# The half copy of a1_rows on GpSimd moved ahead of the product of bias and b1

## The reference

```
x = x + (x @ W.T + bias + (x @ A0[id0].T) @ B0[id0].T)      # W 512x512; A0 32 x 16 x 512; B0 32 x 512 x 16
x = x + (x @ B1[id1].T) @ A1[id1].T                         # B1 8 x 16 x 512;  A1 8 x 512 x 16
```

## Time and profile before

| | |
|---|---|
| median of 3 runs | 102.09 us (100.86 to 102.17) |
| the profiled execution | 100.96 us |
| its span, first to last instruction | 98.8 us |
| mean granted clock of TensorE in the span | 0.983 of full speed |
| busy: PE / PEld / DVE / ACT / POOL | 93% / 92% / 65% / 59% / 59% |

### The profile page before, as it was taken

The page is one execution under the profiler, slowest core; times in us unless marked ns, Lnnn a source line. Parts: engine busy times, 40 slices in busy tenths (PEclk is TensorE's granted clock), DMA queues, the critical chain, the costliest instruction groups (busy, mean ns, idle before and its releaser), DMA issues.

```text
span 98.8 us, 2305 instructions
## 1 busy us (share of the span) xinstructions
PE 92.2 (93%) x662; PEld 91.1 (92%) x662; DVE 64.5 (65%) x120; ACT 58.7 (59%) x189; POOL 57.9 (59%) x126
## 2 busy tenths in 40 slices
PE   5979999999992999999999999999999999999980
PEld 5979989998991999999999999999999999999970
DVE  4499796254172527786876859587876959687360
ACT  0074679695464829695957658494856749490310
POOL 6504003980277999897585958567595957618500
PEclk9999999999999589999999999999999999999999
DMA  1999999927688158979999389995537192620205
GB/s 47 345 360 380 380 338 299 213 55 194 180 231 267 47 133 224 277 288 243 218 234 245 127 209 255 224 251 211 99 141 177 69 239 36 211 106 0 106 0 212
DMA packets 16335, 19.45 MB, mean 197 GB/s; under 512 B 1444, under 2 KB 11556, under 8 KB 16164
## 3 DMA queue, kind: packets, MB, share of 16 engines
q1 hardware_dynamic: 15040, 14.04, 48.0%
q0 software_dynamic: 1280, 5.28, 21.4%
q10 hardware_dynamic: 4, 0.00, 0.0%
HBM read 13.47 MB, written 5.84 MB: 195 GB/s over the span
## 4 chain that ended last, share of the span: by engine, by line
PE 64%; issue 14%; POOL 8%; DMA 8%; SPq 2%; DVE 1%; DVEq 0%; POOLq 0%
PE psum L394 48%; PE psum L440 12%; DMA gathered_rows<-by_rank,rows 4%; PE psum L432 4%; DMA by_rank<-row_ends 3%; SPq L182 2%; POOL a_by_rank L285 2%; POOL bias_b_terms L282 1%; POOL w_chunks L277 1%; DVE y L679 1%; POOL g_sel L332 1%; POOL g_sel L270 0%; DVE y L769 0%; DVEq L44 0%; POOL batch_mask L267 0%
## 5 line engine op out<-in xcount | busy, mean ns | idle before, releaser
L394 PE MATMUL psum<-wd,xt 128*128 128x256 f32 (+1 forms) x384 | 63.2, 314 | 0.0
L394 PEld LDWEIGHTS psum<-wd,xt 128*128 128x128 f32 x384 | 57.0, 191 | 0.0
L558 ACT ACTIVATE wd<-table_rounded 128x128 fp32r x128 | 27.7, 298 | 14.3 <-PE psum L394 12.4
L339 POOL TENSOR_TENSOR up_rows<-gathered_rows,up_rows 128x512 fp32r<-128x512 f32 x16 | 20.7, 1292 | 15.1 <-ACT up_rows L558 15.1
L322 POOL DMA_INDIRECT gathered_rows<-by_rank,rows x16 | 15.9, 994 | 6.8 <-DMA by_rank<-row_ends 4.3
L640 DVE TENSOR_TENSOR xt<-psum,xt 128x512 fp32r<-128x512 f32 x16 | 11.1, 693 | 6.7 <-ACT xt L558 6.7
L440 PE MATMUL psum<-up_rows,u_sel 128*128 128x256 f32 x96 | 14.8, 292 | 0.0
L647 DVE STREAM_TRANSPOSE psum<-x_squares 128x512 f32<-128x512 f32 x13 | 14.4, 1109 | 0.0
L440 PEld LDWEIGHTS psum<-up_rows,u_sel 128*128 128x128 f32 x96 | 13.5, 199 | 0.1
L332 POOL TENSOR_TENSOR g_sel<-gathered_rows,batch_mask 128x16 f32<-128x16 f32 x64 | 12.1, 225 | 0.9 <-DMA gathered_rows<-by_rank,rows 0.6
L558 ACT ACTIVATE xt<-psum 128x512 fp32r<-128x512 f32 x16 | 9.6, 598 | 4.9 <-DVE psum L647 2.2
(11 more groups left out here) (60 smaller groups left out, 71.1 us busy)
## 6 DMA issues: line engine op xcount, KB each, us to landing
out<-y SPq DMA_DIRECT2D x15, 256.0 KB
x_squares<-in_x SPq DMA_DIRECT2D x8, 256.0 KB, 6.1
w_rows<-in_L_cond_base_weight SPq DMA_DIRECT2D x4, 256.0 KB, 3.6
bw_rows<-in_L_cond_lora_B_w SPq DMA_DIRECT2D x1, 1024.0 KB, 6.8
a_rows<-in_L_cond_lora_A_w SPq DMA_DIRECT2D x1, 1024.0 KB, 9.1
by_rank<-bw_by_rank SPq DMA_DIRECT2D x4, 256.0 KB
x_squares<-in_x SPq DMA_DIRECT2D x8, 128.0 KB, 3.2
x_rows<-in_x SPq DMA_DIRECT2D x3, 256.0 KB, 9.2
```

What stands on the lines that cost most here:

```text
L339: nc.gpsimd.tensor_tensor(out=up_rows[:, k % 2, LO, :], in0=gathered_rows[:, k % GATHERS, 0:D], in1=up_rows[:, k % 2, HI, :], op=ALU.subtr ...
L394: last = nc.tensor.matmul(bank_of(k, half)[:, start:end], xt[:, k % 2, c, x_part, :], wd[:, w_part, c, col:col + end - start], start=(c == ...
L558: return nc.scalar.activation(dst, src, ACT.Copy)
```

## The change

On GpSimd the wait for a1_rows and the half copy by rank change places with the waits for the bias and b1 and their product. Nothing else differs.

```diff
             nc.gpsimd.tensor_copy(w_chunks[:, C - 1, :, :],
                                   w_rows[:, C - 1, :].rearrange("p (m c) -> p c m", c=C)).then_inc(w_chunked[C - 1], 1)
 
+            pool.wait_ge(a1_in, 16)
+            nc.gpsimd.tensor_copy(a1_by_rank[:, R // 2:R, :],
+                                  a1_rows[:, :, R // 2:R].rearrange("p o r -> p r o")).then_inc(a1_by_rank_ready, 1)
             pool.wait_ge(bias_in, 16)
             pool.wait_ge(b1_in, 16)
             nc.gpsimd.tensor_tensor(out=bias_b1_terms[:, :], in0=b1_rows[:, :], in1=bias_all[:, :],
                                     op=ALU.mult).then_inc(bias_b1_step, 1)
-            pool.wait_ge(a1_in, 16)
-            nc.gpsimd.tensor_copy(a1_by_rank[:, R // 2:R, :],
-                                  a1_rows[:, :, R // 2:R].rearrange("p o r -> p r o")).then_inc(a1_by_rank_ready, 1)
```

## The result

The changed kernel takes 98.36 us (median of 4 executions, 97.92 to 98.58), the kernel before 102.13 (100.86 to 103.36); ratio 0.9665, 95% interval 0.9568 to 0.9762. Two later comparisons gave 98.35 and 98.38 us with ratios 0.9771 (0.9715 to 0.9828) and 0.9834 (0.9778 to 0.9891). The ratio moves because the kernel before has executions of 99.6 and of 103.7 us, and the comparisons leave out most of the long ones; the experiments take that apart. The profiled execution took 97.92 us, span 95.8, against 100.96 and 98.8: 3.04 us less.

What follows compares the result with a forecast made beforehand. A start-up of about 32 us, then a loop that TensorE fills, was taken as the bound. Hole 1.89 plus clock 2.09 less 0.57 gave 3.41: 100.96 to 97.55 us, forecast 97.9 with part of the spread; range 96.9 to 99.9.

Steps and rivals of the forecast that it cites:

- Where the copy could start: GpSimd's half copy, waiting only for a1_rows, starts at about 14.5 us in place of 17.73.
- The product within 0.1 us of 16.5: GpSimd's product, now behind the copy, still starts near 16.52 us when the bias comes; latest bound 17.15.
- What is late next: ScalarE's copy of g caps the row_ends store on SyncE: issue at about 20.38, 2.02 us earlier, not 2.50.
- Landings unchanged: The row_ends store's landing and gather(0) keep their 3.37 and 4.11 us in their new place.
- A: TensorE's hole shrinks but stays: landing 0.5 to 1.6 us longer in the crowd, clock falls; 99.5 to 100.6 us; chance 0.12.
- D: Slower: DMA crowd makes row_ends store and gather take 6.1 us each; 103.7 us, or 105.8; chance 0.03.
- The hole, 1.89 us: TensorE's idle time before add_gh(0), 29.96 to 31.85, closes, with 0.13 us to spare: 1.89 us gained.
- The clock, 2.09 less 0.57: TensorE's stretch behind the hole runs at full clock: 2.09 us back, less 0.57 lost waiting for GpSimd.
- GpSimd's lateness: TensorE waits for g_sel(1), up_low(1) and g_sel(2) in the first blocks: 0.14, 0.15 and 0.28, together 0.57 us.
- The third of the 1.13 us: Share kept of the 1.13 us between profiled execution and median of runs, taking the forecast from 97.55 to 97.9.
- Rival B: TensorE's hole closes but the clock falls all the same: gain 1.89, 99.1 us; chance 0.08.
- The port that GpSimd and VectorE share: GpSimd's copy beside VectorE costs nothing, at most the 0.23 us of the ids conversion, unneeded before 17.8.

Runs made afterwards that it cites:

- the first run with the hole filled: Kernel before with 13 unused matmuls of zeros on TensorE ahead of add_gh(0): 101.24 us, ratio 1.0079.
- c1: The kernel before, unchanged, run again for its trace and clocks: four executions, 101.83 to 101.97 us, all with a mean clock of 0.983.

## Why the prediction was right, point by point

The forecast was 97.9 us in 96.9 to 99.9, and faster; measured 98.36, against a profiled sum of 97.55 and a profiled execution of 97.92. Between the profiles the gain was 3.04 us where the sum had 3.41: the path and the waits were right, and the term most off was the price of the low clock.

- **Where the copy could start:** forecast 14.5, measured 14.64. Right.
- **The product within 0.1 us of 16.5:** it started at 16.93, since the bias landed later in this execution (0.29 us of wait stand before it, so not the copy held it). In the other traces of this order it started at 16.95 to 17.49, in most of them right behind the copy, which began at 14.80 to 15.44; five are past my latest bound of 17.15. A miss without a price, since the store still went out 0.10 to 0.11 us after ScalarE's copy of g in every one. In the first trace the row sum started at 18.24 and the table subtractions at 20.93, held by ScalarE as before.
- **What is late next:** forecast ScalarE's copy of g, store at 20.38. Measured 20.51, 0.10 after that copy's end. Right, and so was 2.02 in place of 2.50: the store came 1.89 us earlier.
- **Landings unchanged:** store to gather start 4.12 us (4.24 before), gather start to g_sel 4.33 (4.31 before). Right. The crowd of rivals A and D did not reach the row_ends store. Ahead of it, from 20 to 21 us, the DMA engines are now busier (columns as in the earlier trace rows; DMA share 0.57), most likely with the second layer's stores, and that did not lengthen its way to the gather:

```profile
20.00:21.00 1.00, 1.00 (x11) 1.00 (x10) 0.07 (x1) 1.00 (x3) 0.66 (x3) 1.00 0.57 132
```

- **The hole, 1.89 us:** by the chain of waits add_gh(0) starts at 30.09, 1.76 us before 31.85. The hole is closed; the 0.13 us are TensorE itself, whose base group started at 25.27 where the earlier trace rows's execution had it at 25.15.
- **The clock, 2.09 less 0.57:** from add_gh(0) to up(2) the chain went from 9.59 us (31.85 to 41.44) to 8.29 (30.09 to 38.38), 1.30 in place of 1.52. The term that was mis-sized is the clock's. I priced the six base products behind add_gh(0), and the six behind up(0), at the 0.90 us of a later block. They are not the same work: here all six have 384 columns, there three of them have 256. The first row is the changed kernel's at 32 us, the second the kernel before's later block, the last two are from the chain of the first run with the hole filled, at full clock:

```profile
L394 PE MATMUL psum<-wd,xt x6: 336/336/343, 32.0 to 32.8; 128*128 128x384 f32 x6
L394 PE MATMUL psum<-wd,xt x6: 281/312/342, 68.4 to 69.2; 128*128 128x256 f32 x3, 128*128 128x384 f32 x3
...
33.59 1.05 PE psum L394 x6
35.36 1.06 PE psum L394 x6
```

At full clock the stretch takes 0.22 + 1.05 + 0.71 + 1.05 = 3.03 us, not 2.73, so the low clock cost 4.82 - 3.03 = 1.79 us, not 2.09. GpSimd's lateness had the right size. The rest of the way to up(2) takes 4.68 at full clock (0.22, 0.90, 0.71, 0.90, 0.22, 1.73), 7.71 in all, so the changed kernel's 8.29 holds 0.58 us of waiting; I had 0.57. That it fits so closely is partly luck. TensorE comes to add_gh(1) 0.3 us later than I had it, and I left out the step from g_sel's end to add_gh's start, some 0.14 us: g_sel(1) ends at 32.89 and add_gh(1) starts at 33.03. The kernel before had 0.09 us of such waiting itself, and 1.79 + 0.09 - 0.58 is the measured 1.30.
- **Where the argument was too sure, and what was luck:** I took the fall of the clock as part of the hole's fixed price. It is not: it came in 19 of 51 executions of before. With a full clock before takes 100.3 to 100.6, and the change is worth 1.9 to 2.2 us; at a clock of 0.983 some 3.5 (101.9 against 98.4), at 0.963 some 5.2. The profile I summed from had a fall, and the median of the runs shown (their clocks are not on record) stood at the height of executions with one. That is why 4.2 us below that median came out nearly right; in the two later comparisons the gain is 2.3 and 1.7%, not 3.4. From a profile with a full clock the sum would have been about 100.4 - 1.89 = 98.5. The third of the 1.13 us between profile and median was a guess. Between the changed kernel's profile and its median 0.44 us are left, and a spread of 4 us is now 0.9, so the spread went largely with the clock. Why the profiled execution of before took only 100.96, less than any of the other 19 with a fall, is not shown.
- **Rival B,** that the fall has another cause: with the hole filled the clock fell in 1 of 20 executions, in kernels without the hole (the changed one, bias first, 1 us of delay, both gather orders) in 0 of 36, with the hole put back in 5 of 12. So the fall goes with this hole, though not strictly: one execution with the hole filled had it too. The page "TensorE: Matmul & The Clock Gate" of the Trainium skill (What's actually happening) has the rate fall after an idle window. I had read it as speaking for B, in case this hole is not such a window; the counts speak against B all the same. The same section says that the window runs free of the kernel, and that the number of slow matmuls at a kernel's start therefore varies from run to run. That one kernel here has falls in 19 of 51 executions, in its middle as far as they were traced (c1 and the profile of before), fits that, but no run here shows where the window stood.
- **The port that GpSimd and VectorE share:** the conversion of the ids, beside the end of the copy, took 0.36 us in place of 0.23, and ended 0.08 us after the copy did. The second row is the same conversion with the bias loaded first, where the copy runs from 16.08 to 18.03: 1.27 us, ended 0.08 us after the copy again.

```profile
16.37 0.36 DVE L727 TENSOR_SCALAR ids_all_f<-ids_all 128x128 f32<-128x128 int32 x1
...
16.84 1.27 DVE L727 TENSOR_SCALAR ids_all_f<-ids_all 128x128 f32<-128x128 int32 x1
```

In six of the other seven traces of the changed order it took 0.63 to 0.66 us and ended 0.09 us after the copy; in the seventh, where the ids landed only as the copy ended, 0.23. With that the lock of the Trainium skill's page "SBUF — State Buffer" (SBUF: two separate sides) agrees. My price of at most 0.23 us was too low, since the conversion can wait for all that is left of the copy; up to 1.05 us of it was hidden, as nobody needed the result sooner, but for 0.15 us on GpSimd's row numbers with the bias loaded first. VectorE's other operations beside the copy kept 0.68.

## What to carry to other kernels

On an in-order engine a step whose data is there should not stand behind a wait for something loaded later; find such pairs by setting the landing times of loads beside the order of the waits. Then ask which step comes last in the new order, since it caps the gain (here 2.0 of 2.5 us), and whether the engine that waited has its own work up to the new time. Before pricing a low clock from one profile, look at the mean clock of several executions: a hole can cost its length always and the clock only sometimes.

## What the runs showed of the hardware that was not expected

- A hole of 1.8 to 1.94 us on TensorE was followed by a fall from 2.4 to 1.2 GHz in 19 of 51 executions of before and 5 of 12 with the hole put back (told by the mean clock; the two traces with a fall, c1's and the profile of before, show it right behind the hole); with 1.41 us (in the one trace) in 0 of 5. The falls came in clusters (4 of 4 executions in one set, 4 of 17 in another beside it), and one came with the hole filled.
- The 0.87 us between the table's landing and the first gather's start is mostly work that runs beside other GpSimd operations: with a product in between, the gather starts 0.17 us after the product. 1.04 us of products moved g_sel(0) by 0.37 us.
- Gathers issued in the loop at 34.46 and 34.23 us (the two runs with a later gather(3)) took 4.9 and 5.0 us to g_sel, against 4.3 for the first.
- A conversion on VectorE from SBUF to SBUF, 0.22 to 0.23 us alone, took up to 1.27 us beside a GpSimd copy and in eight of nine traces ended 0.08 to 0.09 us after it.
